# ScalarE's order in the top-p attention step: R copies behind the exponential, A·V behind the second level, GpSimd's addition ahead of its bracket

## What is computed

```python
def _top_p_attention(X, W1, W2, W3):
    logits = (X @ W1.T @ W2.T) @ (X @ W3.T).T
    probs = softmax(logits)
    # keep the largest probabilities of each row until their sum reaches 0.9
    mask[rows, idx] = (cumsum(sorted) - sorted) < TOP_P
    A = probs * mask
    return A / A.sum(-1, keepdims=True)

R = adj + I;  R = R / R.sum(-1)
for n in range(2):                     # STEPS
    A = _top_p_attention(Xa, W1, W2, W3)
    Xf = R @ Xf
    Xa = A @ Xa
    Z = Z + Xf @ U1[n].T + Xa @ U2[n].T
h = X + Z                              # then layernorm, and a second layernorm with the input
```

## Time and profile before

| | us |
|---|---|
| median of 3 runs | 4404.75 (4403.72 to 4407.32) |
| profiled execution | 4407.04 |
| its span | 4405.20 |
| busy: PE / DVE / ACT / POOL | 3792.1 / 3624.1 / 3116.2 / 1004.4 |
| granted TensorE clock, mean | 0.935 |

### The profile page before, as it was taken

How to read it: one execution, slowest core, us unless ns; L and a number is a source line. 1 busy time by engine, 2 the same in 40 slices (tenths; PEclk the granted TensorE clock), 3 DMA queues, 4 the chain that set the end, 5 groups by cost and what they waited for, 6 DMA issues and landing times.

```text
span 4405.2 us, 66289 instructions
## 1 busy us (share of the span) xinstructions
PE 3792.1 (86%) x25364; PEld 3171.0 (72%) x25364; DVE 3624.1 (82%) x6399; ACT 3116.2 (71%) x3129; POOL 1004.4 (23%) x1412
## 2 busy tenths in 40 slices
PE   8677777777777769999999679999999999999987
PEld 5677777777777747777777467777777777777776
DVE  2999999999999838888886498777778878898885
ACT  3789898889888845555554477777777777777761
POOL 0000000000000000001011243333333345555664
PEclk8899999999999979999999789999999999999998
DMA  3211111111111020000000212222322332333322
GB/s 116 90 46 63 46 63 46 63 44 65 44 66 44 28 69 14 19 16 19 16 19 17 81 50 90 85 91 91 91 86 82 119 94 88 104 106 106 100 89 86
DMA packets 131760, 292.49 MB, mean 66 GB/s; under 512 B 14123, under 2 KB 94187, under 8 KB 127059
## 3 DMA queue, kind: packets, MB, share of 16 engines
q1 hardware_dynamic: 131410, 287.99, 20.2%
HBM read 250.19 MB, written 37.75 MB: 65 GB/s over the span
## 4 chain that ended last, share of the span: by engine, by line
PE 63%; ACT 15%; issue 10%; POOL 4%; DVE 3%; DMA 2%; SPq 1%; ACTq 0%; POOLq 0%; DVEq 0%
PE ps L717 18%; PE ps L813 18%; PE ps L652 9%; ACT b L884 6%; PE ps L758 5%; PE ps L802 4%; ACT b L878 3%; ACT b L984 3%; PE ps L633 2%; ACT b L872 1%; PE ps L790 1%; PE ps L780 1%; DMA b<-in_adjTb 1%; SPq L293 1%; POOL b L479 1%
## 5 line engine op out<-in xcount | busy, mean ns | idle before, releaser
L717 PE MATMUL ps<-b 128*128 128x257 f32 x4096 | 908.7, 381 | 15.7 <-DMA b<-in_adjTb 15.6
L813 PE MATMUL ps<-b 128*128 128x257 f32 x4096 | 902.2, 380 | 0.0
L652 PE MATMUL ps<-cb,b 128*128 128x128 f32 x4096 | 607.9, 312 | 321.8 <-ACT b L878 321.8
L717 PEld LDWEIGHTS ps<-b 128*128 128x128 f32 x4096 | 777.5, 190 | 138.8 <-DMA b<-in_adjTb 19.5
L813 PEld LDWEIGHTS ps<-b 128*128 128x128 f32 x4096 | 771.6, 190 | 111.6
L652 PEld LDWEIGHTS ps<-cb,b 128*128 128x128 f32 x4096 | 547.3, 163 | 371.2 <-ACT b L878 329.5
L1164 DVE SCALAR_TENSOR_TENSOR b<-b 128x4096 f32<-128x4096 f32 x128 | 566.4, 4425 | 62.2 <-ACT b L872 58.8
L1166 DVE CUSTOM_DVE_ANT_0 b<-b 128x4096 f32<-128x4096 f32 x128 | 566.4, 4425 | 5.6 <-DMA b<-in_adj 1.3
L884 ACT ACTIVATE b<-ps 128x1024 f32<-128x1024 f32 x512 | 500.1, 1022 | 75.1 <-PE ps L652 73.7
L633 PE MATMUL ps<-b 128*64 128x128 f32 x8192 | 503.7, 276 | 0.0
L878 ACT ACTIVATE b<-b 128x4096 f32<-128x4096 f32 x128 | 474.3, 3706 | 8.1 <-DVE b L1168 8.1
(11 more groups left out here) (185 smaller groups left out, 4729.1 us busy)
## 6 DMA issues: line engine op xcount, KB each, us to landing
b<-in_adjTb SPq DMA_DIRECT2D x256, 512.0 KB, 3.9
b<-in_adj SPq DMA_DIRECT2D x32, 2048.0 KB, 8.0
y_d<-b SPq DMA_DIRECT2D x64, 128.0 KB, 1.7
h_d<-b SPq DMA_DIRECT2D x64, 128.0 KB, 1.8
b<-h_d SPq DMA_DIRECT2D x64, 128.0 KB, 2.2
b<-in_xT SPq DMA_DIRECT2D x1, 4096.0 KB, 15.0
b<-in_x SPq DMA_DIRECT2D x32, 128.0 KB, 2.2
b<-y_d SPq DMA_DIRECT2D x32, 128.0 KB, 2.0
```

Source lines behind the costliest of these rows:

```text
L652: last = nc.tensor.transpose(bank(2 * (gq % 3), 2)[:, b * 128:(b + 1) * 128], ub[:, u % UB, j * 128:(j + 1) * 128], ident_s)
L717: last = mm(b[:, 0:XA], aj[:, q % AJR, e, :], xf[:, j, :], start=False, stop=(j == NT - 1))
L813: last = mm(o[:, 0:XA], at[:, q % ATR, b, :], xa[:, j, :], start=(j == 0), stop=(j == NT - 1))
```

## The change

On ScalarE, in `acts`: the copies of A·V and mq go from behind level 1 to behind level 2; the copy of the first R product goes from behind level 2 to behind level 3; the exponential comes next; the copy of the second R product goes from before the exponential to behind it. On GpSimd: `final_add` goes from behind `bracket` to ahead of it. No operation is added, removed or resized; the orders of TensorE and VectorE stay as they are.

```diff
                         if n < NT:
                             levels(n)
+                        if n in fslot:
+                            final_add(fslot[n])
                         if n + 2 < NT:
                             bracket(n + 2)
-                        if n in fslot:
-                            final_add(fslot[n])
...
                     for k in range(1, ACT_LEVELS + 1):
                         if t < NT:
                             level(t, k)
-                        if k == 1:
+                        if k == 2:
                             if 1 <= n <= NT:
                                 av_ev(n - 1)
                             if n >= 2 or n + 3 < NT:
                                 mq_ev(n - 2 if n >= 2 else None, n + 3 if n + 3 < NT else None)
-                        if k >= ACT_LEVELS - 1 and items:
-                            r_ev(items.pop(0))
-                    for r in items:
+                    for r in items[:1]:
                         r_ev(r)
                     if n + 2 < NT:
                         expo(n + 2)
+                    for r in items[1:]:
+                        r_ev(r)
```

## The result

| | before | changed | ratio (95% interval) |
|---|---|---|---|
| median, us | 4404.77 | 4342.78 | 0.9859 (0.9842 to 0.9876) |
| span of the profiled execution | 4405.2 | 4339.3 | |

The account below looks back on a forecast made before the run. TensorE and ScalarE were taken to close each lap in turn, neither full. Early laps -90.4 us, late laps +5.4 and tail -1.4 sum to -86.4, from 4404.75 to 4318 us; range 4300 to 4345 (64%).

Parts of the forecast that it names:

- the circle: Late laps: GpSimd's flags, addition, bracket, ScalarE's levels 1 and 2, norms, all-reduce form a ring of 59.5 us, setting the lap.
- Part 1: Early laps: second R copy goes behind the exponential; lap falls to 52.5 us (bounds 52.3 and 53.7), 90.4 less in all.
- the term of the score slots: TensorE's refill: four score slots at full clock, priced at 2.08/2 each, take 4.2 us of the 8.4 lower bound.
- reloading xf: Early laps: the reload costs 0.5 us once instead of some 5, because bracket and y rows come earlier.
- Part 2: Early laps: A·V and mq copies behind level 2 move the mask's end to 44.1 us, wanted at 52.5, so hidden.
- Part 3: Late laps: the products' later copies close a circle through GpSimd; lap goes from 58.65 to 59.5 us, loss 5.4.
- signs of being wrong: Late laps near 54 us, L717 waiting over 2 us a lap for adjTb chunks, or early L802 waiting for L1373.
- code's return: Late laps, GpSimd behind the all-reduce: return of its ordinary code takes 7.03 us, previously covered by the wait for the exponential.
- rival (b): Late laps: one GpSimd stretch more, because spare wait covered part of the loads; lap 64.0, result 4372 us; chance 13%.
- Part 4: Late laps: addition ahead of bracket ends VectorE's 66 us of waits without helping TensorE; its 1.5 per circle costs 18.
- Tail: Behind the flags of lap 30: last R copy comes after 58.1 us instead of 59.5, gain 1.4.
- my estimate of 4300 from that page: Late laps: with the page's load of about 6 us in both gaps, the circle is 58.0, the result 4300 us.

Follow-up runs that it names:

- R alone: Kernel before with only the second R copy put behind the exponential and the first behind level 3: 4279.6 us, 0.9714 of before.
- Norms first: Changed kernel with GpSimd's norms of finished rows put ahead of the A·V scaling and accumulation: 4241.0 us, 0.9625 of the kernel before.
- P: Copies of A·V and mq put behind level 2; as the only edit to the kernel before: 4436.7 us, 1.0070.
- A: GpSimd's final addition put ahead of the bracket; as the only edit to the kernel before: 4388.8 us, 0.9960.

## Why the prediction was right, and by how much it missed

The mechanism was right, and one term of the circle was too small. That the result lies inside 4300 to 4345 is partly luck: the late laps alone, with the rest as forecast, would have given 4350, and errors of the other sign in the early laps and the tail made up for some of it.

**Part 1, early laps: right, a little too careful.** The forecast lap was 52.5, the measured one 51.6, outside its lower bound of 52.3. The refill is 7.7, not 8.6. Of the 0.9, 0.5 is the term of the score slots. I took 1.04 us a slot from the 2.08 of eight matmuls as the price at full clock, and the row starts at half clock; at full clock four slots take 3.63. Another 0.2 lies in the transposes (3.49, not 3.7), and 0.2 I had put on top of my own lower bound. In all, 16 x 0.9 = 14 us more gain. The kernel before, first the clock (third number from the end) in the row's first half microsecond, then the four slots of the refill of the earlier trace rows:

```profile
3199.34:3199.80 0.46, 0.46 (x4) 0.34 (x2) 0.39 (x3) 0.21 (x1) 0.34 (x2) 0.57 0.00 0
```

```profile
3254.52 5.26 PE ps L758 x16
```

So the 6.7 us that the refill gained are the stop itself, 4.0, and 2.7 of half clock behind it: 5.26 instead of 3.63 for the slots, and 1.97 instead of 0.87 for eight transposes. (ScalarE's own terms add up to 45.4 us, not the 46 that I wrote; nothing hangs on it.)

Against it, reloading xf was to shrink from 5 us to 0.5 and didn't: the lap in which it happens takes 56.5 us, 4.9 more than a plain one. TensorE still waits for y there:

```profile
3352.13 2.23 SPq L293 DMA_DIRECT2D y_d<-b  x2
```

```profile
3359.70 0.67 PE L706 MATMUL ps<-b,cb 128*128 128x257 f32 x2 [3.14 <-DMA b<-y_d]
```

The y rows go out 18.5 us into the lap (24.0 before), but TensorE is ready for them 6.7 us earlier in the lap than before, so it still waits (3.1 us, before 2.1). From the bracket's start to the y rows it is 24.3 us, where it was 18.5, because the bracket's long stretches grew in the early laps too. Of the 4.9 us, 3.1 are the wait for y and 1.3 one for an adjTb chunk. Against the forecast's 0.5, that took back 4.4.

**Part 2, early laps: right.** Nothing of the products' move shows there: laps of 51.6 with it and, in "R alone", without it. VectorE's wait for the flags, 2.7 us a lap (34.5 in 13), is covered by the mask's slack.

**Part 3, late laps: the mechanism right, its size off.** One of my own signs of being wrong did come: waits of L717 for adjTb chunks of 5.6 us a lap, where I allowed 2. I had said that TensorE would idle some 7 us a lap for the mask; it is 1.9 for the mask (23.2 us in 12 laps) and 5.6 for the chunk. "Norms first" shows that most of the chunk's wait follows from the circle, so the circle stands, but the split was wrong. The wait of L1002 for L484 is 7.9 us, where I had about 4. The circle closed where it was said, and experiments with one term of it changed the lap as the theory wants (3.2 us out: 3.2 less; 10.7 out: VectorE's 53.9). Its terms, in the lap shown above and, where it varies, as the mean of twelve:

| term | forecast | lap shown | mean |
|---|---|---|---|
| gap behind the all-reduce ("code's return") | 7.03 | 8.1 | 7.6 |
| addition | 1.5 | 3.6 | 4.2 |
| bracket to square root | 11.42 | 11.2 | 11.2 |
| levels 1 and 2 | 19.15 | 19.2 | |
| copy, scaling, accumulation | 2.8 | 2.7 | |
| norms | 10.74 | 10.6 | |
| all-reduce | 6.86 | 6.3 | 6.5 |
| sum | 59.5 | 61.7 | 62.2 |

The addition is the term that failed. I priced it by the one place without a long stretch in it; in the circle it has one, 2.7 us on average above its own 1.42. That is rival (b) at 60% of its price: a stretch that the spare wait had covered. My argument against (b), that 25 us of idle time cover no more than 13, rested on two laps. The laps between speak against it: in the kernel before, L476 took 4.45 us behind 12.7 us of idle time, 3.56 behind 14.8 and 1.99 behind 18.6. And what matters is the case with no idle time beyond the gap, which no lap of before showed together with a bracket (the shortest idle time there was 12.2). 12 x 2.7 = 32 us more than forecast.

**Part 4: right in sign.** The addition ahead of the bracket costs 14 us in this company (I had said 18 for its 1.5). Its surplus of 2.7 is not its own: with the addition put back, the bracket takes 2.6 us more to its square root. VectorE's waits went and brought nothing.

**Tail.** 6.4 us gained instead of 1.4, 5 more. The last R copy came 53.1 us behind the flags. I had given lap 31 a whole lap of 52.5 behind the mask, but it has no logits left to compute: from the first transposes (4239.07) to the last R copy (4286.51) it takes 47.4.

**Sum.** -86.4, then -14 and +4.4 in the early laps, +32.5 and -1.2 in the late ones, -5 in the tail: -69.7; another 3.7 us lie ahead of E1 and behind the last R copy: -65.9 between the spans, -62.0 between the medians. The Trainium skill (GPSIMD Engine Reference, Instruction dispatch) gives about 6 us for the load at the first call into freshly loaded code. Of the two gaps here, the one ahead of the all-reduce agrees (6.1 us), the one behind it is longer (7.6), and my estimate of 4300 from that page was 43 us off, my own sum 24. The larger part of the miss, the extra stretch inside ordinary instructions, is in neither gap.

Where the time went that the change ought to have given: R is worth 126 us alone, and 64 of them are lost again, nearly all in the late laps, to a circle through GpSimd that P closed and A lengthened.

## What to carry to other kernels

When work on one engine's queue is put later, ask who stands behind it on the *next* engine in order, and add up the whole ring back to the start: its sum is a lower bound of the lap, whatever the busy shares say. Here GpSimd was busy 26% of the span and set the pace, and the cure was not less work but moving 10.7 us of it into a wait that the ring had anyway. Price work put right behind an all-reduce of GpSimd by a case in which it has no idle time ahead beyond the gap itself, or take one stretch more into the sum. And take the price of an instruction at full clock only from a row whose granted clock you have read.

## What was not expected of the hardware

- Behind a partition all-reduce GpSimd shows 7.6 us on average with no instruction, and then long stretches booked on ordinary instructions: L476, 0.28 us where it is short, takes 2.3 to 4.4; L479 4.54; L482 4.60. Their sum is about the same whichever work comes first. As means of twelve laps it is 2.8 + 4.3 + 4.5 with the addition in front (the 2.8 is what it takes above its own 1.42), 2.6 + 4.5 + 4.6 with the bracket in front and the addition behind it, and 3.0 + 4.5 + 4.6 with the addition ahead of the all-reduce. That this is code being fetched is an inference from their place; no run shows the fetch itself, nor that of the gaps.
- TensorE waited 5.6 us per late lap for a DMA chunk without the lap depending on it. It fell to a quarter when the ring was shortened: the chunk was issued behind rows that GpSimd makes, so the wait was a branch of the same ring.
